# Head attention of a four-layer fused kernel: where the side jobs of TensorE sit between the key tiles

## The reference

```python
x = x + _L0_xattn_ref(_layernorm(x, axis=-1), ctx_2048, mask, mask, Wq, bq, Wk, bk, Wv, bv)
x = x + _L0_ffn_ref(_layernorm(x, axis=-1), weight1, weight2, weight3)
x = x + _L1_xattn_ref(_layernorm(x, axis=-1), mask2, ctx_2048, ctx_2048, wq, wk, wv, wo)
x = x + _L1_ffn_ref(_layernorm(x, axis=-1), w1, w2, w3)
...
def _L0_xattn_ref(target, source, target_mask, source_mask, Wq, bq, Wk, bk, Wv, bv):
    q = jnp.einsum('oc,bct->bot', Wq, target) + bq[None, :, None]
    k = jnp.einsum('oc,bcs->bos', Wk, source) + bk[None, :, None]
    v = jnp.einsum('oc,bcs->bos', Wv, source) + bv[None, :, None]
    ...
    dot = jnp.einsum('bhdt,bhds->bhts', q, k) / math.sqrt(HEAD_DIM)
    mask = target_mask[:, :, :, None] * source_mask[:, :, None, :]
    dot = mask * dot - (1.0 - mask) * NEG
    amap = jax.nn.softmax(dot, axis=-1) * mask
    out = jnp.einsum('bhts,bhds->bhdt', amap, v)
    return out.reshape(b, HEADS * HEAD_DIM, t)
```

## Time and profile before

| what | before |
|---|---|
| median of 3 executions | 1445.33 us |
| the profiled execution, device time | 1449.05 us |
| its span in the profile | 1447.2 us |
| PE busy | 1314.5 us (91%) |
| DVE busy | 1019.0 us (70%) |
| ACT busy | 649.7 us (45%) |
| POOL busy | 297.0 us (21%) |

### The profile page before, as it was taken

One profiled execution on the slowest core, in us unless ns is written; L12 is line 12 of the kernel. 1 busy time (PEld: TensorE's weight loads), 2 busy tenths in 40 slices (PEclk: granted clock), 3 DMA queues, 4 the chain that ended last, 5 costly groups with the idle time before them and its releaser, 6 DMA issues.

```text
span 1447.2 us, 23348 instructions
## 1 busy us (share of the span) xinstructions
PE 1314.5 (91%) x9142; PEld 753.9 (52%) x9142; DVE 1019.0 (70%) x1523; ACT 649.7 (45%) x941; POOL 297.0 (21%) x473
## 2 busy tenths in 40 slices
PE   5788868898988989886999989999999999999998
PEld 2344412222222222222767767787777777777776
DVE  8999778889898897884777856644467544575353
ACT  5776537777787877783453111232111321112210
POOL 1018255545455554220000000000000000000000
PEclk9999969999999999996999999999999999999999
DMA  6300222333334323232744301000010000100000
GB/s 201 106 18 23 73 70 91 109 88 101 106 93 147 99 81 101 62 122 67 267 129 143 104 30 59 13 18 1 30 60 2 30 1 15 63 12 30 1 1 30
DMA packets 78038, 101.23 MB, mean 70 GB/s; under 512 B 14679, under 2 KB 51647, under 8 KB 77927
## 3 DMA queue, kind: packets, MB, share of 16 engines
q1 hardware_dynamic: 75879, 99.43, 21.8%
q0 software_dynamic: 2048, 0.27, 0.1%
HBM read 78.07 MB, written 21.34 MB: 69 GB/s over the span
## 4 chain that ended last, share of the span: by engine, by line
PE 39%; DVE 9%; DMA 2%; ACT 1%; issue 1%; POOL 1%; POOLq 0%; DVEq 0%; ACTq 0%; SPq 0%
PE double L1800 13%; PE double L1814 11%; PE double L1826 5%; PE double L1879 3%; PE double L1847 3%; PE double L1836 2%; PE double L1866 1%; DVE stats L1987 1%; PE double L1784 1%; DVE f1w L2092 1%; DVE hid L2034 1%; DMA x_early<-scr_x 1%; DVE gate L2032 1%; DMA out_x<-x_early 1%; DVE x_early L2003 1%
## 5 line engine op out<-in xcount | busy, mean ns | idle before, releaser
L1029 ACT ACTIVATE prob<-level,head_scale 128x512 f32<-128x512 f32 x512 | 319.2, 683 | 92.4 <-PE level L946 92.2
L1390 DVE TENSOR_REDUCE nmx<-level 128x2 f32<-128x1024 f32 x256 | 304.9, 1221 | 56.3 <-PE level L936 56.0
L1912 ACT ACTIVATE th<-double 128x512 f32<-128x512 f32 x96 | 54.0, 563 | 384.7 <-PE double L1800 211.6
L946 PE MATMUL level<-stacks 59*128 59x512 f16 x512 | 175.0, 390 | 24.5 <-ACT prob L1029 24.2
L936 PE MATMUL level<-stacks 57*128 57x512 f16 x512 | 150.7, 394 | 11.6 <-DVE nmx L1390 10.9
L374 PE MATMUL level<-prob,x_parts 128*128 128x512 bf16 x540 | 126.4, 389 | 34.9 <-DVE prob L421 18.0
L1800 PE MATMUL double<-x_parts,f0w 128*128 128x256 f16 x1408 | 156.3, 274 | 1.6 <-PEq L521 1.6
L1973 POOL TENSOR_TENSOR rstd<-meanvar,halfpow 128x2 f32<-128x2 f32 x22 | 15.2, 691 | 689.7 <-DVE meanvar L1993 689.7
L1800 PE MATMUL double<-x_parts,f1w 128*128 128x256 f16 x1408 | 155.2, 273 | 0.9 <-DVE hid L2034 0.9
L1800 PEld LDWEIGHTS double<-x_parts,f0w 128*128 128x128 bf16 x1408 | 138.2, 98 | 20.3 <-issue 2.1
L1800 PEld LDWEIGHTS double<-x_parts,f1w 128*128 128x128 bf16 x1408 | 137.6, 98 | 18.9 <-DVE hid L2034 1.2
(11 more groups left out here) (254 smaller groups left out, 1878.3 us busy)
## 6 DMA issues: line engine op xcount, KB each, us to landing
stacks<-scr_q SPq DMA_DIRECT2D x64, 96.0 KB
stacks<-scr_k SPq DMA_DIRECT2D x64, 96.0 KB
hid<-in_f1w1t SPq DMA_DIRECT2D x8, 704.0 KB, 6.7
hid<-in_f1w2t SPq DMA_DIRECT2D x8, 704.0 KB, 4.2
inputs<-in_x SPq DMA_DIRECT2D x8, 512.0 KB, 7.3
inputs<-in_ctx SPq DMA_DIRECT2D x8, 512.0 KB, 7.0
scr_q<-splits SPq DMA_DIRECT2D x16, 256.0 KB, 2.4
scr_k<-splits SPq DMA_DIRECT2D x16, 256.0 KB, 2.1
```

Of the source, the lines that this page charges most:

```text
L946: nc.tensor.matmul(pB[n % 2], Ks[rows, g, j // 2, P * c:P * (c + 1)], Qs[rows, g, j // 2, :], start=True, stop=True).then_inc(s["b_pe"], 1)
L1029: nc.scalar.activation(prob[:, c, j, :], pB[(64 * b + 16 * g + 4 * c + j) % 2], ACT.Exp, scale=hscale[:, 10:11]).then_inc(s["exp_done"], 1)
L1390: nc.vector.tensor_reduce(nmx[:, g % 2, :, half, tt], pA[(32 * b + 8 * g + u // 2) % 2], AX.X, ALU.max, negate=True).then_inc(s["max_done" ...
L1912: y = nc.scalar.activation(th[:, 0:m, :], src[:, 0:m, 0:S], ACT.Tanh, scale=0.5 / XS)
```

## The change

The table of side jobs is rewritten, so that q, k and v stand alone, each in half 0 of a key tile of its own, and o, o move one key tile later. The evacuations on ACT and DVE, the splits on POOL and two steps of SyncE's queue are moved to fit. Nothing is computed otherwise.

```diff
         MISC = {
-            (0, 0): [("q", 0, 1), ("k", 0, 1)], (0, 1): [("nm", 1, 0), None], (0, 2): [("t", 3, -1), None],
-            (0, 3): [("o", 0, -1), ("o", 1, -1)],
-            (1, 0): [("q", 1, 1), ("k", 1, 1)], (1, 1): [("nm", 2, 0), None], (1, 2): [("t", 0, 0), None],
-            (2, 1): [("nm", 3, 0), None], (2, 2): [("t", 1, 0), None], (2, 3): [("v", 0, 1), ("v", 1, 1)],
-            (3, 1): [("nm", 0, 1), None], (3, 2): [("t", 2, 0), None],
+            (0, 0): [("q", 0, 1), None], (0, 1): [("nm", 1, 0), None], (0, 2): [("t", 3, -1), None], (0, 3): [("k", 0, 1), None],
+            (1, 0): [("o", 0, -1), ("o", 1, -1)], (1, 1): [("nm", 2, 0), None], (1, 2): [("t", 0, 0), None],
+            (1, 3): [("q", 1, 1), None],
+            (2, 0): [("k", 1, 1), None], (2, 1): [("nm", 3, 0), None], (2, 2): [("t", 1, 0), None], (2, 3): [("v", 0, 1), None],
+            (3, 0): [("v", 1, 1), None], (3, 1): [("nm", 0, 1), None], (3, 2): [("t", 2, 0), None],
         }
+
+        PROJECTED = {(0, 0): (0, 0), (0, 3): (0, 1), (1, 3): (1, 0), (2, 0): (1, 1)}
...
                 if not last:
+                    fill(b + 1, 1)
                     store_parts(b + 1, 1)
-                    fill(b + 1, 1)
-                if not last:
                     fill(b + 1, 2)
...
                         exps(b, g, c, 0)
-                        if c == 0 and g < 2 and not last:
-                            q_evac(b + 1, g, (0,))
+                        if (g, c) in PROJECTED and not last:
+                            i, n = PROJECTED[g, c]
+                            q_evac(b + 1, i, (n,))
...
                         exps(b, g, c, 1)
-                        if c == 0 and g < 2 and not last:
-                            q_evac(b + 1, g, (1,))
...
                 for g in range(NG):
-                    if not last and g < 2:
-                        split(b + 1, g, (0,))
+                    if not last and g == 0:
+                        split(b + 1, 0, (0,))
+                    if not last and g == 2:
+                        split(b + 1, 1, (1,))
...
                     if not last and g < 2:
-                        split(b + 1, g, (1,))
+                        split(b + 1, g, (1 - g,))
                     if g == 1 and not ending:
                         ln_pow(b + 2)
...
-                            if g == 0 and c == 3 and not first:
+                            if g == 1 and c == 0 and not first:
                                 residual(b - 1, (half,))
...
-                            if g == 2 and c == 3 and not last:
-                                v_evac(b + 1, half)
+                            if (g, c) in ((2, 3), (3, 0)) and half == 0 and not last:
+                                v_evac(b + 1, g - 2)
```

## The result

The change makes the kernel slower: 1459.42 us in the median of 6 runs (1457.40 to 1465.22) against 1445.12 in 6 runs of the kernel before (1442.60 to 1448.98). The ratio is 1.0103, with a 95% interval of 1.0091 to 1.0116. The forecast was 1439.7, so it has the wrong sign, and the result lies outside its range. The profiled execution after took 1459.25, the one before 1449.05, which is slower than all six of its runs here: the two profiles differ by 10.2, the medians by 14.3.

A forecast was written before the change was run, and what follows sets the result against it. No engine was full; waits between engines set the stage. Sequences 1 to 5 give -1.6, sequence 6 -5.2, sequence 0 +1.2, sequence 7 0: in all -5.6, from median 1445.33 to 1439.7 us; 80% range 1426 to 1450.

The forecast's parts named there:

- `rstd` was late: In (1, 3), the layer norm's power stands behind q's split on POOL, so DVE waits 3.2 us for `rstd`.
- Rival 2: DVE's L1334 passes POOL's L1102: stall 2.0 per sequence, no fall of the clock, 1427 in all; chance 0.13.
- Rival 3: PE's gains are absent, as DVE makes tiles with projections late by another 0.5 to 1: 1445; chance 0.14.
- rival 4: The layer norm's power does not wait behind the split of q: no stall, 1415; chance 0.05.
- the row of L81: POOL's one-element L81 took 0.36 instead of 0.2 beside DVE's L1334; read as the two excluding each other.
- the price of the clock: A fall behind the idle in (2, 1) costs 0 to 2.9 us; 0.9 taken, within the stall of 4.1.
- Wait and exclusion: Late power plus L1334 held by L1102 make tile (2, 1) 3.2 us longer, in sequences 0 to 5.
- rival 1: Clock at half through (2, 1) and (2, 2) for 6.8 us: 2.9 for 0.9 in six sequences, 1451.7; chance 0.18.
- (1, 0) with POOL taken as free: (1, 0) with o, o takes 4.42 and (1, 1) 3.55, DVE coming 1.3 us late behind the statistics.
- the 2.9 of sequence 0: Sequence 0, starting at half clock and without o, gains 2.9 from its projections; with the stall of 4.1, +1.2.
- -4.42: Gain per sequence from spreading q, k, v and o over the key tiles, before the layer norm's stall.

The follow-up runs named there:

- experiment 3: The changed kernel plus 12 matmuls of 512 columns on PE in the stall of (2, 1), their result overwritten unread: 1444.01 us.
- Experiment 5: Experiment 1's kernel with the layer norm's statistics behind (1, 1) instead of (0, 3), and the power between value_group and the split of q: 1411.18 us.
- experiment 1: The changed kernel with the layer norm's power at the head of group 1 on POOL, ahead of the split of q: 1426.1 us.
- experiment 2: The changed kernel with only the split of k, i = 1, moved behind the DMAs of the maxima and value_group in group 2: 1455.39 us.

## Why the prediction was wrong

**Right.** The structure held, most of it to a tenth. `rstd` was late by 3.19 for 3.2. DVE's L1336 stood behind L1102, 2.41 for the pair. Tiles (0, 0) and (0, 3) of sequence 6 took 3.48 and 3.53, (1, 3) 3.53, (2, 0) 3.76, (2, 3) and (3, 0) 3.49, for 3.48 each and 3.84, and the sequence 53.33 for 53.3. PE waited for no fill in the change. *Rival 2*, L1334 passing L1102, is refuted. The same L1336 that takes 0.54 alone took up to 1.49 beside L1102. *Rival 3*, no gains on PE, and *rival 4*, no wait, are refuted by sequence 6 and by the six waits.

**A reading that failed beside it: the rate of L1334.** The prediction took 0.54 us for 512 elements as one element a cycle, and so held that by the Trainium skill L1334 would pass. The division leaves out that an instruction has a fixed part. Rows of the kernel before, by shape (count, then busy us, mean ns of one, and idle us before):

```profile
L2033 DVE TENSOR_SCALAR hid<-gate 128x512 f16<-128x512 f32 x40 | 17.1, 427 | 1.4
L2033 DVE TENSOR_SCALAR hid<-gate 128x256 f16<-128x256 f32 x8 | 2.4, 294 | 0.3
L2025 DVE TENSOR_TENSOR hv<-gate,double 128x512 f32<-128x512 f32 x40 | 27.5, 687 | 1.4
L2025 DVE TENSOR_TENSOR hv<-gate,double 128x256 f32<-128x256 f32 x8 | 3.4, 420 | 0.3
```

For 256 elements more, the tensor_scalar L2033 takes 0.13 us more and the tensor_tensor L2025 0.27: tensor_scalar goes at twice the rate. L1334 shows the same: without the 0.17 that a tensor_scalar of two elements takes (L1237), its 0.54 leaves 0.37 for 510 elements, 0.73 ns each, where L2025 takes 1.04 ns each. By the Trainium skill (SBUF — State Buffer, section Who interferes with whom) a VectorE instruction with at most one SBUF input contends with GpSimd only in a two-port mode, and tensor_scalar is among those that can be in one. The trace agrees: L1336 was held, and it ended 0.29 behind L1102, about the 0.27 that 512 elements take at the rate of L2033 (an estimate). So the Trainium skill, read with these rows, stood with the row of L81 and against rival 2.

**The step that failed first: the price of the clock.** The prediction said "I take 0.9, as a fall of 3.4 us lies two thirds over idle time". It lies over little: PE resumes at 422.04, at 422.54 the clock goes to 0.50, and it stays there for 6.83, with PE idle for 0.96 of them. The price is 2.2 per stall, by experiment 3. Wait and exclusion together were forecast at 3.2 and cost 3.5. So a stall is 5.7, for 4.1 forecast, and rival 1 (its point of decision was 5.1) had this mechanism right, with 2.9 for the clock, its upper end.

**The step that failed second: (1, 0) with POOL taken as free.** "In (0, 3) ... the statistics hold DVE 1.67 us more" took its duration from a place where POOL was doing nothing. In the change the split of k runs there, and L1239 takes 0.99. The rule needed for this stood in the prediction, used for L1334, and was not applied to the other DVE steps that meet a split at its new place. (1, 0) and (1, 1) came to 5.15 + 3.42 where 7.97 was forecast: +0.6. Worse, in sequences 0, 2 and 4 the clock falls there too, for which the prediction had no term; in sequence 4 behind a wait for the load of x, of which it had none either. Experiment 5 takes all of this away and gains 14.9 on experiment 1.

**The sum**, for sequences 0 to 6 of the profiled executions. Forecast 405.3, measured 423.9, difference 18.6:

```
clock behind the stall, 1.3 more in six         8.0
wait and exclusion, 0.3 more in six             1.8
(1, 0) and (1, 1) at full clock, 0.6 in five    3.0
falls of the clock at (1, 0) to (1, 2) and, in
  sequence 4, the late load: 2.6, 1.5, 2.7      6.8
sequence 0: its tiles gave 4.2, for 2.9        -1.35
left                                            0.3
```

For the 2.9 of sequence 0 the prediction gives no tiles; those of the other sequences give 4.1 without o, o. And the terms as written for sequence 6, -4.42 and -1.0 from 58.49, give 53.07. Its 53.3 comes out only with the 0.26 by which (2, 3) of that sequence is shorter than the others before (4.91 for 5.17), which the prediction does not mention.

Sequence 7 and the end of the stage took about 3.6 less than before, where the forecast had 0; this gives some of it back. Why sequence 7 gained was not looked into. What stays open too is why the falls at (1, 0) and (1, 1) come in some sequences only: in the change in 0, 2 and 4, in experiment 1 in 0, 3, 4 and 5, in experiment 3 in 0 and 3. Idles of 1.43 and 0.95 or 0.96 led to one in sequence 2 of the change and to none in its sequences 1, 3 and 5.

**And the chances.** The exclusion was argued from one small row, against a reading of the Trainium skill that was itself wrong, and held. The clock had a row as well: half a clock right behind an idle, for 3.4, with PE at work. Reading "0 to 2.9" off it and taking a value near the low end was a choice that the row did not back. That the two other stalls of PE were ruled out by one stretch with an idle of 1.51 at full clock was too little: experiment 2 shows a fall behind 1.60.

## What to carry to other kernels

When work moves on an in-order queue, list what stands behind it for another engine: here one `ln_pow` of 0.72 behind a split of 3.4 turned a gain of 18 us into a loss of 14, and moving two lines gave it back. Then lay the moved GpSimd instructions beside everything that VectorE does at that time, tiny steps too, since each VectorE tensor_scalar that meets one costs up to the rest of it. And count an idle of TensorE, one of 1.6 us too, not by its own length only but with the slow work that can follow; where the idle can't be removed, work that nobody reads can be cheaper than none.

## What the runs showed of the hardware

- **The clock fell behind short idles.** In experiment 2 a PE idle of 1.60, mostly with one of 0.95 close behind, was followed by a granted clock of 0.50 (1.2 GHz), in six of six sequences. Idles of 1.43 and 0.95 in the change were followed by one in one sequence of four, and idles of 0.61 and 0.96 in its sequence 0 were too. Behind the stall of 3.00 a fall cost 2.2 us beyond its stall. With PE kept busy in the same stall (12 unread matmuls, 2.76 us) it stayed at 1.00, and the kernel was 15.4 us faster. The Trainium skill (TensorE: Matmul & The Clock Gate, section HAM oscillation — how this bites in real kernels) tells of waits of about 3 to 5 us for a DMA that bring the clock down again and again in a loop. The falls here came once or twice in a sequence as well, but behind shorter idles, of 3.00 and less, so a reader should not take gaps of that length as the least that matters.
- **DVE tensor_scalar with one SBUF input is held by POOL, even when tiny.** 128x2 took 0.99 for 0.17 and ended 0.02 behind the POOL instruction that it met, 128x16 took 2.04 for 0.17 and ended 0.03 behind, and 128x512 took 1.49 for 0.54 and ended 0.29 behind, about what its own 512 elements take (0.27, the estimate above).
- **Where 2.6 us of statistics stand can be worth fifteen.** Experiment 5 removed no work. Sequences 1 and 2, which had kept their clock in experiment 1, went from 55.1 to 53.6. Those in which it had fallen, up to 57.7, came down to between 53.6 and 53.8, and sequence 0 to 54.84, as none of them lost the clock any more. Together that is 16.2 us of the two profiled executions, which differ by 15.7.
